# Midpoint products: VectorE moves them out of their bank and ScalarE squares them from memory, for tiles 10 to 16

## The reference, cut to what matters

```python
XW = mobius_matvec(W, X)
AXW = weighted_midpoint_lincomb(A_hat, XW)
return expmap0(jax.nn.relu(logmap0(AXW)))

def mobius_matvec(W, x):
    x_norm = _norm(x)
    mx = x @ W
    mx_norm = _norm(mx)
    res = _tan_k(mx_norm / x_norm * _artan_k(x_norm)) * (mx / mx_norm)
```

## Time and profile before

| | before |
|---|---|
| median of 3 runs | 2429.38 us |
| lowest, highest | 2427.58, 2431.55 us |
| the profiled execution | 2422.31 us |
| its span | 2420.5 us |
| mean granted clock of TensorE | 0.974 |
| PE busy | 2254.0 us, 93% |
| DVE busy | 1714.5 us, 71% |
| ACT busy | 1569.5 us, 65% |

### The profile page before, as it was taken

One profiled execution on the slowest core, in us unless ns is written; L12 is line 12 of the kernel. 1 busy time (PEld: TensorE's weight loads), 2 busy tenths in 40 slices (PEclk: granted clock), 3 DMA queues, 4 the chain that ended last, 5 costly groups with the idle time before them and its releaser, 6 DMA issues. The chain is left out here.

```text
span 2420.5 us, 69264 instructions
## 1 busy us (share of the span) xinstructions
PE 2254.0 (93%) x29240; PEld 1467.8 (61%) x29240; DVE 1714.5 (71%) x3030; ACT 1569.5 (65%) x2621; POOL 35.4 (1%) x44
## 2 busy tenths in 40 slices
PE   7979999999999787999999968899989899999999
PEld 4535555555555457999999953355567545555554
DVE  5847888888887678999999975832467334556684
ACT  3438888888888568999999957522345444444552
POOL 1210000000000000000000000000000000000000
PEclk9989999999999898999999989999999999999999
DMA  4022222223222552121211225011121334334441
GB/s 176 9 80 66 84 84 84 84 88 101 93 84 78 175 202 73 34 52 52 52 52 40 73 64 178 13 37 37 37 76 44 94 94 121 104 108 126 117 127 36
DMA packets 224469, 201.05 MB, mean 83 GB/s; under 512 B 148972, under 2 KB 181906, under 8 KB 219964
## 3 DMA queue, kind: packets, MB, share of 16 engines
q1 hardware_dynamic: 222604, 189.11, 25.9%
q10 hardware_dynamic: 1584, 7.93, 1.0%
HBM read 145.37 MB, written 51.46 MB: 81 GB/s over the span
## 5 line engine op out<-in xcount | busy, mean ns | idle before, releaser
L1464 ACT ACTIVATE m_above<-keep_u,m_nvs 128x1408 fp8e5<-128x1408 f32 x318 | 435.6, 1454 | 0.0
L968 PE MATMUL m_acc<-keep_z_hi,m_p_hi 128*128 128x448 f16 x968 | 338.0, 353 | 19.5 <-DVE m_p_lo L852 16.5
L968 PE MATMUL m_acc<-keep_z_hi,m_p_lo 128*128 128x448 f16 x924 | 326.2, 353 | 0.0
L968 PE MATMUL m_acc<-keep_z_lo,m_p_hi 128*128 128x448 f16 x924 | 324.8, 352 | 0.0
L1805 PE MATMUL m_acc<-right_x_all,m_b 128*128 128x64 f16 x3872 | 240.5, 194 | 18.3 <-DVE m_b L1521 16.3
L1805 PE MATMUL m_acc<-right_x_all,m_c 128*128 128x64 f16 x3872 | 237.8, 194 | 16.6 <-DVE m_c L1529 12.8
L1805 PEld LDWEIGHTS m_acc<-right_x_all,m_b 128*128 128x128 fp8e5 x3872 | 231.3, 99 | 21.0 <-DVE m_b L1521 17.5
L1809 PE MATMUL m_acc<-right_x_all,m_b 128*128 128x64 f16 x3696 | 239.4, 194 | 2.2 <-issue 2.0
L1805 PEld LDWEIGHTS m_acc<-right_x_all,m_c 128*128 128x128 fp8e5 x3872 | 227.5, 99 | 19.3 <-DVE m_c L1529 14.9
L1809 PE MATMUL m_acc<-right_x_all,m_c 128*128 128x64 f16 x3696 | 236.5, 193 | 1.1 <-issue 1.1
L1809 PEld LDWEIGHTS m_acc<-right_x_all,m_b 128*128 128x128 fp8e5 x3696 | 228.2, 99 | 2.0 <-issue 1.8
(11 more groups left out here) (417 smaller groups left out, 5759.0 us busy)
## 6 DMA issues: line engine op xcount, KB each, us to landing
m_at<-adjT SPq DMA_DIRECT2D x11, 1408.0 KB, 7.3
m_at<-adjT SPq DMA_DIRECT2D x11, 1280.0 KB
keep_u<-rows SPq DMA_DIRECT2D x16, 704.0 KB, 4.3
low<-m_lw SPq DMA_DIRECT2D x32, 256.0 KB, 5.3
at<-edge_at SPq DMA_DIRECT2D x22, 352.0 KB, 3.2
keep_at<-at ACTq DMA_DIRECT2D x11, 704.0 KB, 6.4
keep_at_first<-at SPq DMA_DIRECT2D x22, 352.0 KB, 3.4
p_x_all<-x SPq DMA_DIRECT2D x4, 1536.0 KB, 9.5
```

Of the source, the lines that this page charges most:

```text
L968: return pe.matmul(acc[:, n % 3, s, of], part(m, q, s, low), z[:, m % T, s, of], start=first, stop=last, skip_group_check=True)
L1464: last = act.activation(above[:, q % RA, j - j0], u[:, g % RU], ACT.Relu, bias=nvs[:, g // NB, j:j + 1], scale=STEEP, saturate=False)
```

## The change

For tiles 10 to 16 (`MOVED`) ScalarE's copy of the product goes. VectorE does it instead, a tensor_scalar with the same scale from the bank into the same memory, counted by a new semaphore `moved`. ScalarE's square of these tiles waits for `moved` and reads the copy in memory, with scale 1.0, instead of the bank. The products of t + 2 wait for `moved` instead of the square, since the move is now the last reader of the bank. Two waits for all seven moves stand ahead of later readers of the rows.

```diff
+        moved = kit.sems("moved")[0]
...
+        MOVED = range(EA - 2, EA + 5)
...
                 def products(t):
                     pe.wait_ge(lo_made, t + 1)
-                    if t >= 2:
+                    if t - 2 in MOVED:
+                        pe.wait_ge(moved, t - 1 - MOVED[0])
+                    elif t >= 2:
                         pe.wait_ge(msq_made, t - 1)
...
                 def finish(t):
                     act.wait_ge(mx_done, t + 1)
-                    act.activation(mx[:, t, :], main[:, t % 2, :], ACT.Copy, scale=1 / WS).then_inc(mx_made, 1)
+                    if t not in MOVED:
+                        act.activation(mx[:, t, :], main[:, t % 2, :], ACT.Copy, scale=1 / WS).then_inc(mx_made, 1)
                     if t >= 2:
                         act.wait_ge(msq_made, t - 1)
-                    act.activation(sq[:, t % 2, 1, :], main[:, t % 2, :], ACT.Square, scale=1 / WS,
+                    if t in MOVED:
+                        act.wait_ge(moved, t + 1 - MOVED[0])
+                    of, by = (mx[:, t, :], 1.0) if t in MOVED else (main[:, t % 2, :], 1 / WS)
+                    act.activation(sq[:, t % 2, 1, :], of, ACT.Square, scale=by,
                                    accum_out=ssq[:, 1, t:t + 1]).then_inc(msq_made, 1)
...
                     act.wait_ge(co_made, 1)
+                    act.wait_ge(moved, len(MOVED))
                     for t in range(EA, T):
...
                         if EA <= t < EA + 5 and next(chains[0], "made") == "made":
                             dve.sem_inc(g_made, 1)
+                        if t in MOVED:
+                            dve.wait_ge(mx_done, t + 1)
+                            dve.tensor_scalar(mx[:, t, :], main[:, t % 2, :], 1 / WS, None, ALU.mult).then_inc(moved, 1)
+                        if t == X_AT[0]:
+                            dve.wait_ge(moved, len(MOVED))
                         if t in X_AT:
```

## The result

| | before | after |
|---|---|---|
| median | 2428.48 us (4 runs) | 2444.81 us (4 runs) |
| lowest, highest | 2424.77, 2431.55 us | 2442.66, 2446.50 us |
| the profiled execution | 2422.31 us | 2446.50 us |
| its span | 2420.5 us | 2444.7 us |

The ratio is 1.0075, 95% interval 1.0061 to 1.0088. The change makes the kernel 16.3 us slower by the medians; the forecast was 15.6 us, and 2445.0 us for the median.

A forecast was written before the change was run, and what follows sets the result against it. No engine was taken as full; TensorE, ScalarE and VectorE hand tiles round in a circle. Stretch +14.4 us and clock +1.2 make +15.6, median 2445.0 us, range 2438 to 2452.

The forecast's parts named there:

- The place of the wait: Steps 10 to 16: product ready about 0.3 us after VectorE's low part starts, so the move stands behind that low part.
- the circle: ScalarE and VectorE in steps 10 to 16: closed within one tile, 4.04 us without small work, where 3.4 were.
- The chain's pieces: VectorE's factor-chain work in steps 13 to 16, 1.98 to 2.56 us each, ahead of the move; these steps carry some 11 us.
- The size of each step: Steps 10 to 16: 4.04 us each plus 13.33 of small work, 41.61 us where 27.17 were.
- The waits forecast for VectorE: VectorE's waits for ScalarE's high parts in the changed steps: not gone, some 2.7 us in every step.
- The move's price: Each of VectorE's seven moves from product bank to memory: 0.68 us, from a 677 ns row of the first stage.
- The clock: TensorE's clock falls between slow tiles; hidden for products 13 to 16, on products 18 0 to 2.3 us, taken as 1.2.
- Rival A: Lower clock comes back in products of 18, 19 and 20: 6.8 us on top of 14.4, +21.2, 2450.6; chance 0.13.
- Carried whole to the end: From high part 18 on, old order and no slack, so the whole delay reaches the end.
- the 2.4 allowed: From high part 18 to the first block's end: same length as before within 2.4 us.
- Rival B: Only the move is exposed, chain work stays hidden: seven steps grow by 0.64, 4.5 us, 2433.9; chance 0.05.
- Rival C: ScalarE is the bound and idle VectorE takes the copy: 0.49 back per step, 3.4 us, 2426.0, not slower; chance 0.04.

The follow-up runs named there:

- e5: Kernel before without any move, but ScalarE's copies of tiles 10 to 16 wait until VectorE passes the place of the change's move; 2439.33 us, ratio 1.0050.
- e4: The change with only tiles 13 to 16 moved instead of 10 to 16; 2442.99 us, ratio 1.0064 to the kernel before.
- e1: The change with VectorE's move directly behind low part t+1, ahead of the step's small work and chain piece; 2431.84 us, ratio 1.0021 to the kernel before.
- e7: The change plus twelve extra matmuls in each of TensorE's steps 15 to 18 to keep it busy; 2440.81 us, ratio 1.0067 to the kernel before.
- e12: Kernel before with ScalarE instead of VectorE making the high rows of tiles 6 to 11, no move; 2423.82 us, ratio 0.9995.
- e8: The change with the move directly behind low part t+1 and ScalarE's square and answers one step later; 2425.63 us, ratio 1.0001 to the kernel before.
- e3: The change with only tiles 10 to 12 moved instead of 10 to 16; 2428.60 us, ratio 1.0010 to the kernel before.
- e6: Kernel before, but for tiles 10 to 16 ScalarE squares its own copy from memory, no move; 2427.19 us, ratio 1.0005.

## Why the prediction was right

By its own steps:

- **The place of the wait.** The prediction said that the product is ready 0.3 us after the low part has started, that the move therefore comes behind it, and that the circle closes within one tile. The waits after and e5 show the circle: 13.2 us from the wait alone. The 0.3 us held for the kernel before only. Once the steps are longer the product is made well before the next low part (4.3 us in step 14), and it is VectorE's order alone that keeps the move behind it.
- **The chain's pieces.** They were to carry most of the cost of steps 13 to 16. e4 has 12.6 us for these four steps, and e1, which only moves the piece behind the move, takes back 10.3 of the 15.7.
- **The size of each step.** Worked out were 4.27, 4.44, 4.40, 7.45, 7.91, 6.54 and 6.60 us for steps 10 to 16, together 41.61; measured 4.43, 4.41, 4.55, 7.76, 8.23, 6.65 and 6.81, together 42.84. The term that was too small is the hand-over. From the move's start to the square's start the trace has 0.80 us (1502.76 to 1503.56 in step 10), where I had 0.71: I took the 0.03 us between a high part and its low part, and here it is about 0.1 us, seven times. The rest are the gaps between the chain and the move (0.16 us in step 14) and between the square and the table load, and a small operation of ScalarE's ahead of the normalise in step 10 (0.10), which I left out. The waits forecast for VectorE, some 2.7 us in every step, were 2.8 to 2.9 in the short steps and behind steps 15 and 16, but 4.34 behind steps 13 and 14: the answer with its table load, which the sum has, was left out of that line. The upper end of the forecast should read 16.7, not 16.8.
- **The move's price.** 0.68 forecast, 0.681 to 0.693 measured:

```profile
L2338 DVE TENSOR_SCALAR right_rel<-m_main x7: 681/691/693, 1502.8 to 1541.3; 128x512 f32<-128x512 f32 x7
```

  One row of another stage with the same operation, source and shape gave it to 0.02 us. The Trainium skill's "VectorE: DVE Perf Modes", section "The perf-mode tier table", allows up to twofold speed for any PSUM operand. In these seven rows that is not there for float32: the estimate that the prediction made from it was 0.39 us.
- **The clock.** Taken as 1.2 us, between 0 and 2.3, in products 18 alone; measured 1.6 us, and e7 shows that it is the clock and that nothing else of it is on the path up to there. What I did not see is the lower clock in the first block, which is a term of its own: it held 3.4 us after TensorE's long wait before (from 1556.18) and 5.6 us after (from 1580.84), which is the 0.9 us between 29.57 and 30.47. e7, with the same products, had 29.58. Rival A, in which the lower clock would come back in the products of 19 and 20, did not happen.
- **Carried whole to the end.** The last product is 15.67 + 1.58 = 17.25 us later, TensorE's first matmul of the first block 17.3, and the first copy out of the block 18.2. From the first block to the last one the kernel takes 189.6 us, 189.7 before. From high part 18 to the first copy it is 46.6 us for 44.1, just over the 2.4 allowed. The delay was carried, but the reason named for it was not the one that holds: the second chain does not start when the square of tile 21 is made. VectorE is at its rows for 7.3 us past the start of the last product's copy, and the chain follows without idle time:

```profile
1535.67 0.60 ACT L2148 ACTIVATE right_rel<-m_main 128x512 f32<-128x512 f32 x1 [2.46 <-PE m_main L162]
...
1542.61 0.43 DVE L2272 TENSOR_SCALAR keep_xs_lo<-right_rel 128x512 f16<-128x512 f32 x1
1542.95 0.17 DVE L209 TENSOR_SCALAR m_ssq<-m_ssq 128x20 f32<-128x20 f32 x1
```

  These rows are of the kernel before. So there was slack behind the square of tile 21, and work could be taken off VectorE there, as e12 did with 2.3 us.

Rival B, only the move exposed, fell with e4 (12.6 us in steps 13 to 16, not 2.6). Rival C, ScalarE's relief, fell with the result; e8 shows a condition under which its mechanism works, namely that ScalarE does not need the move in the same step.

One thing stays open. The traces have the first block 18.2 us later, in both profiles of the change; the medians have 16.3 and 13.7 us. The one profile of the kernel before had a short first block (29.57, where most of the experiments have 30.0 to 30.6 us), which would take off up to 1 us. The rest of the kernel varies too, whatever the edit: the start of the stretch lies anywhere from 1493.0 to 1501.3 us in these profiles, and from the first block's copy to the end it takes 852.7 to 857.3 us (855.3 before, 853.9 and 854.0 in the two of the change). So a few runs give a median that is uncertain by some us. I didn't find what sets these lengths. So the closeness of 15.6 and 16.3 is partly luck: the stretch was sized at 15.6 and is 17.3 to the first block's first matmul and 18.2 to its copy.

## What to carry to other kernels

Before an idle engine is given work, look at which side of its waits the work's input arrives: VectorE idled 13.1 us in seven waits here, all of them ahead of a low part, and the product came behind its start. A result that another engine takes in the same step closes a circle between the two, and all that stands ahead of it in the first engine's order, however small, is then on the path; taken one step later, the same instruction cost next to nothing (42.8 us, 32.6 with the move in a better place, 22.8 with the late square). And a mark that runs ahead of the work it stands for shows gains that are given back later, so read the next mark too.

## What I had not expected of the hardware

The spell of lower clock after a long wait of TensorE, ahead of the first block, was 3.4 us in one profile and 5.6 in another of the same matmuls. These rows show the wait, and the windows behind them the clock (length, busy, granted clock, DMA), before:

```profile
1556.18 0.61 PE L2075 MATMUL m_main<-keep_xs_lo,keep_at_first 128*128 128x512 f16 x1 [5.79 <-DVE keep_xs_lo L2272]
...
1556.00:1559.00 3.00, 2.82 (x10) 0.50 0.02 5
1559.00:1562.00 3.00, 3.00 (x19) 0.89 0.00 0
```

and after:

```profile
1580.84 0.61 PE L2079 MATMUL m_main<-keep_xs_lo,keep_at_first 128*128 128x512 f16 x1 [7.19 <-DVE keep_xs_lo L2281]
...
1580.00:1583.00 3.00, 2.16 (x8) 0.50 0.03 5
1583.00:1586.00 3.00, 3.00 (x13) 0.50 0.00 0
1586.00:1589.00 3.00, 3.00 (x21) 0.93 0.00 0
```

The waits were not the same: 5.79 us before and 7.19 after. The three profiles with a wait of 5.6 to 5.8 us (before, e3, e7) have spells of 3.4 to 4.1 us, the eleven with 7.1 to 7.2 us have 4.1 to 5.9, e6 among them (5.1), which has all of its rows and products as before. So one wait of 7.2 us was followed by a spell of 4.1 us in one run and of 5.9 in another, and no run here parts what sets it. That is up to 1 us of the kernel's time that no edit here has asked for, and it is as large as some of the gains that were looked for. The hand-over from VectorE to ScalarE, from a move's end to the square's start, was about 0.1 us, and from ScalarE's high part to VectorE's low part 0.03.
